# Expert tiles as float16 pairs in a kernel that joins a delta-rule attention and a mixture of experts

## The chip, the cores and the metric

The kernel runs on one core of one Trainium2 chip. The metric is the device time of the whole program in microseconds (us), lower is better. A core has five engines with instruction streams of their own: TensorE (PE in the profile, its weight loads PEld), VectorE (DVE), ScalarE (ACT), GpSimd (POOL) and SyncE (SP), and 16 DMA engines that they share. [...]

## The reference

The input x is 2 batches of 2048 rows of 256 numbers, float32. What is computed:

```
xn = layernorm(x)                                  # rows of 256
q, k, v, g = xn@Wq, xn@Wk, xn@Wv, xn@Wg            # 4 heads, DK = 128, DV = 64
k = k / |k| ; q = q * DK**-0.5 ; beta = sigmoid(xn@Wb)
S_t = S_{t-1} + k_t (beta_t (v_t - k_t^T S_{t-1}))^T ;  o_t = q_t^T S_t    # per batch and head
s = (rmsnorm(o) * norm_w * silu(g)) @ Wo
e = argmax(softmax(xn @ router_w^T))               # one of 8 experts for each row
h = relu(xn @ expert_fc[e])**2                     # 1024 wide
y = h @ expert_proj[e]^T                           # 256 wide
out = x + s * silu(y)
```

## The kernel before, in words

**The recurrence.** Each batch is cut into 16 chunks of 128 rows. A chunk is worked on for both batches b and all heads together. `K`, `Q` and `VG` project it, with both operands held as pairs of float16 numbers (high and low part), three matmuls for each product. From k come its transpose (`kT`), the product `G`, and from that X, the strictly upper part of a 128 by 128 matrix for each head (`X32`, `X_h`, and `X_l` on GpSimd). The inverse of the unit triangle 1 + X is built in six levels: each level is `L` and `Dm` and `T` on TensorE, with `Pm_` and `dM` on VectorE and `dZ` on ScalarE between them, for b = 0 and b = 1 in turn. M and Z are the inverse and its transpose. `MZ` and `Zo` on VectorE and `M0` on TensorE set them up: `MZ` copies the identity into M, and `M0` then writes its even columns. At the end of the levels `F`, `Fr_` and `Zc` correct the inverse by one Newton step; `Fr_` adds `ImM`, which is identity minus M and comes from GpSimd. Then `KS`, `U`, `O` and `dS` carry the state S from chunk to chunk, and `ogT_` and `wo` finish the rows.

**The experts.** The 4096 rows are sorted by expert into NT = 39 tiles of 128 rows, a tile having one expert. For a tile, `load_weights` on SP fetches both weight matrices, 1 MB each in float32, into one of three buffers (RING = 3): tile j is fetched once tile j-3 is done. `rows` on GpSimd gathers the rows, TensorE transposes them, and `expert_tile` multiplies: 16 matmuls of 128 columns, then relu and square on ScalarE (`relu`, `sq`), then 8 matmuls of 256 columns. All of that is float32. A float32 matmul stands in the trace as two instructions. `keep_y`, `y_sigmoid`, `gate_y` and `send_y` finish a tile and scatter it into a DRAM scratch, y_d.

**The order.** Nothing is scheduled at run time. Each engine has its order written out by hand: `ramp` (normalisation, routing, the first chunk and its first three tiles), then a step for each chunk i, which holds the levels of chunk i, the state of chunk i-1 and the projections of chunk i+1 with two or three expert tiles dealt out between them by `experts(n)`: seven steps with three tiles (`step3`, i = 1 to 7), five with two (`step2`, i = 8 to 12), and `tail` for chunks 13 to 15 and the last five tiles. `experts(n)` issues n sixteenths of a tile. At the end y_d is read back (wts<-y_d), and `weigh` and `add_x` make the output.

The order of one level and its neighbours in `step2`, for TensorE:

```
L(i, 4) ; wo(i - 1) ; Dm(i, 4) ; experts(2) ; T(i, 4) ; experts(1) ; L(i, 5) ; experts(1) ; Dm(i, 5) ; experts(1)
```

Lines that the rows name: L509 and L520 are the matmuls of an expert tile (`expert_tile`), L539, L555 and L589 are `K`, `Q` and `VG`, L614 is `M0`, L629, L638 and L647 are `L`, `Dm` and `T`, L659, L660 and L668 are `F` and `Zc`, L731 is `wo`, L483 to L485 are the three products of a pair. L1164 is `sq`, L1132 a step of splitting the attention's weights, L1728 is `q_l`, L1768 the identity copy of `MZ`, L2440 is `k_l`, L2446 is `X_l`, L2466 is `ImM_`. L372 is SP's load of the first half of x for the output.

## Time and profile before

| | |
|---|---|
| median of 3 runs (lowest to highest) | 783.77 us (781.04 to 786.33) |
| the profiled execution, its own time | 784.05 us |
| its span, first to last instruction | 782.3 us |
| busy: PE, DVE, POOL, ACT | 722.2, 542.5, 396.9, 354.2 us |
| mean granted TensorE clock | 0.994 of full speed |
| moved by DMA | 116.33 MB |

Busy time of TensorE counts an instruction from its start to its modelled end, and instructions overlap. What an instruction costs the engine is therefore read from the distance between the starts of neighbours. The span divides into a ramp, up to the start of step 3 at 213 us, five steps of three tiles, five of two tiles, and a tail. From step 2 on, one step with three tiles follows the other at a distance of 47.67 us; the steps with two tiles follow at 40.17 us.

### The profile page before, as it was taken

Reading aid. Unit: us, or ns where it says so; the run is one execution under the profiler, and the core shown is the slowest. Engines: PE = TensorE matmul, PEld = TensorE weight load, DVE = VectorE, ACT = ScalarE, POOL = GpSimd, SP = SyncE. Lnnn points to the kernel's source line nnn. Section 1 sums busy time; section 2 is a strip of 40 time slices with the busy share of each in tenths; the row PEclk is TensorE's granted clock in tenths of the full one; section 3 lists DMA queues with packets and bytes.
Section 4 is the critical chain, followed back from the end, with each engine's and each line's share of the span. In section 5 each row is a group of like instructions: output and inputs, shape, how many; then the busy total and the mean of one; then the engine's idle time right before and its main releaser. Section 6 shows DMA issues by size and latency. Waiting matters only on the chain.

```text
span 782.3 us, 23109 instructions
## 1 busy us (share of the span) xinstructions
PE 722.2 (92%) x9442; PEld 621.6 (79%) x9442; DVE 542.5 (69%) x1169; ACT 354.2 (45%) x768; POOL 396.9 (51%) x411
## 2 busy tenths in 40 slices
PE   5666899999999999999999999999999999999976
PEld 4555798878889788887888878888888887979853
DVE  4779457566575665756556577877777777787788
ACT  5551354445444454444445344444444453545432
POOL 3571538354473545626454354647464646545351
PEclk9998999999999999999999999999999999999999
DMA  9420973452335434343354333333333323323076
GB/s 300 145 83 1 386 287 143 153 213 116 130 129 197 162 115 176 134 177 130 116 204 152 131 130 116 128 115 126 116 129 116 129 116 129 131 108 103 22 232 220
DMA packets 37753, 116.33 MB, mean 149 GB/s; under 512 B 3664, under 2 KB 24400, under 8 KB 27664
## 3 DMA queue, kind: packets, MB, share of 16 engines
q1 hardware_dynamic: 33904, 104.62, 36.7%
q0 software_dynamic: 3744, 10.23, 3.9%
q8 instruction: 76, 1.25, 0.7%
q14 instruction: 29, 0.24, 0.1%
HBM read 101.33 MB, written 13.50 MB: 147 GB/s over the span
## 4 chain that ended last, share of the span: by engine, by line
PE 68%; DVE 13%; POOL 7%; issue 6%; DMA 3%; ACT 2%; SPq 0%; DVEq 0%; POOLq 0%
PE bank L509 17%; PE bank L520 16%; PE bank L589 4%; PE bank L483 4%; PE bank L485 3%; PE bank L484 3%; PE bank L555 3%; PE bank L629 2%; PE bank L647 2%; PE bank L638 2%; PE bank L731 2%; PE bank L539 2%; POOL XTl L2446 2%; PE bank L568 2%; DVE M L1768 2%
## 5 line engine op out<-in xcount | busy, mean ns | idle before, releaser
L520 PE MATMUL bank<-wts,hT 128*128 128x256 f32 x624 | 170.9, 393 | 0.0
L509 PE MATMUL bank<-xsT,wts 128*128 128x128 f32 x1248 | 166.0, 281 | 1.2 <-DMA wts<-in_pj 1.1
L509 PEld LDWEIGHTS bank<-xsT,wts 128*128 128x128 f32 x1248 | 150.6, 192 | 4.7 <-DMA wts<-in_pj 1.2
L1785 DVE TENSOR_TENSOR Pm<-bank,lvl_mask 128x256 f16<-128x256 f32 x180 | 68.1, 417 | 62.6 <-PE bank L629 61.9
L520 PEld LDWEIGHTS bank<-wts,hT 128*128 128x128 f32 x624 | 105.4, 191 | 7.3
L2446 POOL TENSOR_TENSOR XTl<-f_t,XTh 128x512 f16<-128x512 f32 x32 | 40.0, 1257 | 125.6 <-DVE XTh L1723 125.4
L1215 ACT CAST Z<-bank 128x256 f16<-128x256 f32 x180 | 59.3, 376 | 96.7 <-PE bank L647 96.6
L1796 DVE TENSOR_TENSOR M<-bank,M 128x256 f16<-128x256 f32 x180 | 68.8, 418 | 38.7 <-PE bank L638 37.8
L1160 ACT ACTIVATE hT<-bank 128x512 f32<-128x512 f32 x78 | 46.7, 599 | 46.9 <-PE bank L509 46.9
L2466 POOL TENSOR_TENSOR ImM<-ident,M 128x512 f32<-128x512 f16 x30 | 35.1, 1189 | 42.1 <-DVE M L1796 42.1
L555 PE MATMUL bank<-xT,wq 128*128 128x128 f16 x768 | 49.3, 222 | 4.1 <-DVE qT16l L1728 3.6
L555 PEld LDWEIGHTS bank<-xT,wq 128*128 128x128 f16 x768 | 45.8, 99 | 5.8 <-issue 3.9
L1164 ACT ACTIVATE hT<-hT 128x512 f32<-128x512 f32 x78 | 49.3, 632 | 1.1
L2440 POOL TENSOR_TENSOR k16l<-f_t,k16h 128x512 f16<-128x512 f32 x32 | 38.1, 1205 | 20.4 <-DVE k16h L1709 20.4
L2419 POOL TENSOR_TENSOR y_sb<-y_sb,y_sg 128x256 f32<-128x256 f32 x39 | 29.5, 757 | 36.5 <-ACT y_sg L1179 36.3
L589 PE MATMUL bank<-wvg,xT 128*128 128x512 f16 x192 | 46.7, 379 | 0.7 <-DVE qT16l L1728 0.7
L539 PE MATMUL bank<-wk,xT 128*128 128x512 f16 x192 | 46.2, 379 | 1.0 <-DVE xT L1609 1.0
L2423 POOL DMA_INDIRECT y_d<-y_sb,to_row x39 | 41.1, 1053 | 8.6 <-issue 5.7
L1768 DVE COPY M<-ident 128x512 f16<-128x512 f16 x30 | 26.7, 889 | 26.4 <-PE bank L485 25.2
L2410 POOL DMA_INDIRECT xs<-xn_d,from_row x39 | 40.5, 1037 | 6.8 <-issue 5.6
L2397 POOL TENSOR_TENSOR root<-beta,up_half 128x8 f32<-128x8 f32 x16 | 29.1, 1821 | 28.5 <-DVE gate L1743 16.2
L1716 DVE TENSOR_TENSOR f_t<-bank,up_neg 128x512 f32<-128x512 f32 x32 | 21.8, 684 | 30.6 <-PE bank L485 30.6
(257 smaller groups left out, 1975.5 us busy)
## 6 DMA issues: line engine op xcount, KB each, us to landing
wts<-in_fc SPq DMA_DIRECT2D x39, 1024.0 KB, 4.9
wts<-in_pj SPq DMA_DIRECT2D x39, 1024.0 KB, 8.4
wts<-in_x SPq DMA_DIRECT2D x10, 512.0 KB, 8.2
wts<-y_d SPq DMA_DIRECT2D x4, 1024.0 KB, 9.6
out_x<-wts SPq DMA_DIRECT2D x16, 256.0 KB, 2.8
xn_d<-wts SPq DMA_DIRECT2D x3, 1024.0 KB, 4.4
x_first<-in_x SPq DMA_DIRECT2D x4, 512.0 KB, 16.4
wts<-in_x SPq DMA_DIRECT2D x4, 256.0 KB, 3.5
```

Of the source, the lines that this page charges most:

```text
L509: ins = pe.matmul(psum[bank[n]][:, (c % 4) * P:(c % 4 + 1) * P], fcw[r][:, k, c * P:(c + 1) * P], xsT[:, k, :], start=(k == 0), stop=(k == ...
L520: ins = pe.matmul(psum[bank[0]][:, 0:D], hT[:, c, :], pjw[r][:, c, :], start=(c == 0), stop=(c == HC - 1))
L539: ins = pe.matmul(psum[KG_BANK[b]][:], xT[:, a, zx, b, k, :], wk16[:, zw, k, :], start=(k == 0 and zx + zw == 0), stop=(k == KC - 1 and zx ...
L555: ins = pe.matmul(bank4(QV_BANK)[:, h, :], wq16[:, zw, k, h * DK:(h + 1) * DK], xT[:, a, zx, b, k, :], start=(k == 0 and zx + zw == 0), st ...
L589: ins = pe.matmul(psum[QV_BANK][:], xT[:, a, zx, b, k, :], wvg16[:, zw, k, :], start=(k == 0 and zx + zw == 0), stop=(k == KC - 1 and zx = ...
L1160: act.activation(half(n), psum[H_BANK[j % 2 ^ n]][:], ACT.Relu).then_inc(relu_ok[n], 1)
L1164: act.activation(half(n), half(n), ACT.Square).then_inc(sq_ok[n], 1)
L1215: act.copy(evens(h4(Zs[last(m)], b), s, 1), half4(level_bank(m, b)).rearrange("p h (n c) -> p h n c", c=s)).then_inc((last_dZ_ok if last(m ...
L1768: dve.tensor_copy(h4(Ms[last(m)], b), ident16[:].unsqueeze(1).to_broadcast([P, H, P]))
L1785: dve.tensor_tensor(h4(Pms[last(m)], b).rearrange("p h (n c) -> p h n c", c=s), half4(level_bank(m, b)).rearrange("p h (n c) -> p h n c", ...
L1796: dve.tensor_tensor(evens(h4(Ms[last(m)], b), s), half4(level_bank(m, b)).rearrange("p h (n c) -> p h n c", c=s), evens(h4(Ms[last(m)], b) ...
L2446: pool.tensor_tensor(h4(XT[1][a % 2], b), h4(f32_t, b), h4(XT[0][a % 2], b), ALU.subtract).then_inc(Xl_ok[b], 1)
```

## The change

1. **Tiles in float16 pairs.** From tile T16 = 9 on (30 of 39 tiles) each float32 product of an expert tile becomes three products of float16 halves: 48 matmuls of 128 columns and 24 of 256 columns. The rows are split when they are kept (ScalarE the high part, `rows_low` on VectorE the low one). After relu, ScalarE makes the high part of h by a square written as float16 (`h_high`) beside the float32 square (`sq`), and GpSimd the low part (`h_low`).
2. **Weights split once.** All expert weights are split during the ramp, in 32 units of 128 by 1024 numbers (512 KB in, 512 KB out). ScalarE issues the load, makes the high part and issues the store (`unit_load`, `unit_high`, `unit_store`), VectorE makes the low part (`unit_low`); the result is in a DRAM scratch w16_d, from which tiles 9 to 38 are fetched, again 1 MB twice. Two units are under way at a time, in the space of x_first. SP therefore loads the first half of x for the output only when all units are stored, right before the fetch for tile 9.
3. **The unit triangle.** `X32` writes by a predicated copy into a tile `unit` that holds the identity, so X comes with its diagonal; `F` then yields M + XM, and `Fr_` is identity minus that, with no `ImM_`. `P32` no longer waits for `X_l`.
4. **M0 whole.** `M0` multiplies by the whole identity (128 columns for each head where there were 64), `M0c` keeps all of it, and the identity copy of `MZ` is gone.
5. **New orders.** The ramp now holds chunks 0 to 2 and nine tiles; `step3` runs for chunks 3 to 7, `step2` for 8 to 12, and every order is written anew.

```diff
-        FIRST_TILES, STEPS = 3, [3] * 7 + [2] * 5
+        FIRST_TILES, FIRST_STEP, STEPS = 9, 3, [3] * 5 + [2] * 5
...
+        w16_d = scratch("w16_d", [E, P, 2, 2, KC * HD], F16)
...
                 def load_weights(j):
                     ex = sp.value_load(tile_e[0:1, j:j + 1], min_val=0, max_val=E - 1)
+                    if j >= T16:
+                        for m in range(2):
+                            sp.dma_start(w16[j % RING][:, m], w16_d[bass.ds(ex, 1), :, m].rearrange("a p z n -> p (a z) n")
+                                         ).then_inc(wt_in[j % RING], 16)
+                        return
...
-                sp.wait_ge(wl_ok, len(W_ORDER))
+                for j in range(RING, T16):
+                    At(sp, j - RING).on(yp)
+                    load_weights(j)
+                for z in range(2):
+                    sp.wait_ge(unit_kept[z], 16 * UNITS // 2)
                 xf = x_first.rearrange("p c (b d) -> p b c d", b=B)
...
-                for j in range(RING, NT):
+                for j in range(T16, NT):
...
+                            else:
+                                ins = pairs(o, [fcw16[r][:, z, k, c * P:(c + 1) * P] for z in range(2)],
+                                            [xsT16[:, z, k, :] for z in range(2)], start=(k == 0), stop=(k == KC - 1))
...
+                        for zh in range(2):
+                            for c in range(HC):
+                                if c % 4 == 0 and zh == 0:
+                                    pe.wait_ge(hh_ok[c // 4], HH_FROM[c // 4] + j - T16 + 1)
+                                if c % 4 == 0 and zh == 1:
+                                    pe.wait_ge(hl_ok[c // 4], HL_FROM[c // 4] + j - T16 + 1)
+                                for zw in range(2 - zh):
...
+                                    ins = pe.matmul(psum[bank[0]][:, 0:D], h16[:, zh, c, :], pjw16[r][:, zw, c, :],
+                                                    start=(n == 0), stop=(n == 3 * HC - 1))
...
-                            ins = pe.matmul(half4(level_bank(m, b))[:, h, :], Zs[last(m)][:, H * b + h, :],
-                                            evens(ident16[:].unsqueeze(1), 1)[:, 0].rearrange("p n c -> p (n c)"),
+                            ins = pe.matmul(bank4(level_bank(m, b))[:, h, :], Zs[last(m)][:, H * b + h, :], ident16[:],
                                             start=True, stop=True)
...
+                def unit_load(u):
+                    if u < 2:
+                        act.wait_ge(wl_ok, W_ORDER[("wk", "wq")[u]])
+                    else:
+                        act.wait_ge(unit_lo, u - 1)
+                    act.dma_start(unit_in[u % 2], unit_of(u)[0]).then_inc(unit_read[u % 2], 16)
+
+                def unit_high(u):
+                    act.wait_ge(unit_read[u % 2], 16 * (u // 2 + 1))
+                    if u < 2:
+                        act.wait_ge(wl_ok, W_ORDER[("wbr", "wvg")[u]])
+                    else:
+                        act.wait_ge(unit_kept[u % 2], 16 * (u // 2))
+                    act.activation(unit_out[u % 2][:, 0], unit_in[u % 2], ACT.Copy, scale=W_SCALE).then_inc(unit_hi, 1)
+
+                def unit_store(u):
+                    act.wait_ge(unit_lo, u + 1)
+                    act.dma_start(unit_of(u)[1], unit_out[u % 2]).then_inc(unit_kept[u % 2], 16)
...
+                def h_high(j, n):
+                    At(act, j).on(relu_ok[n])
+                    act.activation(h16[:, 0, 4 * n:4 * n + 4, :].rearrange("p c n -> p (c n)"), half(n), ACT.Square,
+                                   scale=H_SCALE).then_inc(hh_ok[n], 1)
...
+                def unit_low(u):
+                    dve.wait_ge(unit_hi, u + 1)
+                    dve.scalar_tensor_tensor(out=unit_out[u % 2][:, 1], in0=unit_in[u % 2], scalar=W_SCALE,
+                                             in1=unit_out[u % 2][:, 0], op0=ALU.mult, op1=ALU.subtract).then_inc(unit_lo, 1)
+
+                def rows_low(j):
+                    if T16 <= j < NT:
+                        At(dve, j).on(xsT_ok)
+                        dve.tensor_tensor(xsT16[:, 1].rearrange("p k n -> p (k n)"), psum[H_BANK[j % 2]][:, 0:KC * P],
+                                          xsT16[:, 0].rearrange("p k n -> p (k n)"), ALU.subtract).then_inc(xsl_ok, 1)
...
-                    dve.tensor_tensor(h4(f32_t, b), bank4(KG_BANK[b]), up_neg[:].unsqueeze(1).to_broadcast([P, H, P]),
-                                      ALU.mult).then_inc(X32_ok[b], 1)
+                    fr.on(Gp[b])
+                    fr.on(Xl_ok[b], Xh_ok[b], back=1)
+                    dve.copy_predicated(h4(unit, b), up_strict[:].bitcast(I32).unsqueeze(1).to_broadcast([P, H, P]),
+                                        bank4(KG_BANK[b])).then_inc(X32_ok[b], 1)
...
+                def h_low(j, n):
+                    At(pool, j).on(sq_ok[n])
+                    pool.wait_ge(hh_ok[n], HH_FROM[n] + j - T16 + 1)
+                    cs = slice(4 * n, 4 * n + 4)
+                    pool.tensor_tensor(h16[:, 1, cs, :], hT[:, cs, :], h16[:, 0, cs, :], ALU.subtract).then_inc(hl_ok[n], 1)
...
-                def ImM_(m, b):
```

Three places of the new orders follow, each before and after.

**TensorE, from level 0 of a step with three tiles.** Before, the second product of a tile (`wts,hT`, 256 columns, float32), level products and `Q` of the next chunk:

```order
L629 MATMUL bank<-M,XTh 128x64 x8
L520 MATMUL bank<-wts,hT 128x256 x4
L638 MATMUL bank<-Pm,Z 128x64 x8
L520 MATMUL bank<-wts,hT 128x256
L555 MATMUL bank<-xT,wq 128x128 x24
```

Now the same part of the first such step, where the second product is on float16 halves (`wts,h`):

```order
L566 MATMUL bank<-wts,h 128x256 x3
L687 MATMUL bank<-M,XTh 128x64 x8
L614 MATMUL bank<-xT,wq 128x128 x24
L566 MATMUL bank<-wts,h 128x256 x3
L696 MATMUL bank<-Pm,Z 128x64 x8
```

`Q` stands between `L` and `Dm` now, and each piece of a tile is three short matmuls.

**GpSimd, in a step with three tiles.** Before: `k_l`, gathers (L2410), `X_l`, gating of y (L2419), `ImM_` (L2466), scatters (L2423), `P_l` (L2452):

```order
L2440 TENSOR_TENSOR k16l<-f_t,k16h 128x512 x2
L2410 DMA xs<-xn_d,from_row 128x256
L2446 TENSOR_TENSOR XTl<-f_t,XTh 128x512 x2
L2410 DMA xs<-xn_d,from_row 128x256
L2419 TENSOR_TENSOR y_sb<-y_sb,y_sg 128x256 x2
L2423 DMA y_d<-y_sb,to_row 4480x256
L2466 TENSOR_TENSOR ImM<-ident,M 128x512 x2
L2397 TENSOR_TENSOR root<-beta,up_half 128x8
L2419 TENSOR_TENSOR y_sb<-y_sb,y_sg 128x256
L2423 DMA y_d<-y_sb,to_row 4480x256 x2
L2452 TENSOR_TENSOR PTl<-f_t,PTh 128x512 x2
```

Now, from the gating of the step's first tile on:

```order
L3040 TENSOR_TENSOR y_sb<-y_sb,y_sg 128x256
L3034 TENSOR_TENSOR h<-hT,h 128x512 x3
L3040 TENSOR_TENSOR y_sb<-y_sb,y_sg 128x256
L3034 TENSOR_TENSOR h<-hT,h 128x512
L3025 DMA xs<-xn_d,from_row 128x256
L3073 TENSOR_TENSOR PTl<-f_t,PTh 128x512
L3040 TENSOR_TENSOR y_sb<-y_sb,y_sg 128x256
L3067 TENSOR_TENSOR XTl<-unit,XTh 128x512
L3073 TENSOR_TENSOR PTl<-f_t,PTh 128x512
L3044 DMA y_d<-y_sb,to_row 4480x256 x2
L3067 TENSOR_TENSOR XTl<-unit,XTh 128x512
```

`h_low` (L3034) is new, six times in a step; `ImM_` is gone, and `X_l` (L3067) has moved to the end.

**ScalarE, in the ramp, around level 3 of chunk 0.** Before, relu (L1160) and square (L1164) of a tile, `dZ` (L1215), `kTc` (L1191):

```order
L1215 CAST Z<-bank 128x16x16 x2
L1204 ACTIVATE gate<-bank 128x256
L1160 ACTIVATE hT<-bank 128x512
L1164 ACTIVATE hT<-hT 128x512
L1191 COPY kT_1<-bank 128x1024
L1160 ACTIVATE hT<-bank 128x512
```

Now:

```order
L1440 CAST Z<-bank 128x16x16
L1349 DMA w_d<-x_first 128x2x1024
L1375 ACTIVATE hT<-bank 128x512
L1337 DMA x_first<-in_fc 128x1024
L1375 ACTIVATE hT<-bank 128x512
L1440 CAST Z<-bank 128x16x16
L1429 ACTIVATE gate<-bank 128x256
L1349 DMA w_d<-x_first 128x2x1024
L1385 ACTIVATE hT<-hT 128x512
```

Stores (L1349) and loads (L1337) of units stand between the copies that the levels wait for; each of them, and each `unit_high` (L1345), waits for something of its own.

## Rows read from the trace of the kernel before

**Rows 1.** The page, part 1: busy us, share of the span, instructions of each engine.
```profile
PE 722.2 (92%) x9442; PEld 621.6 (79%) x9442; DVE 542.5 (69%) x1169; ACT 354.2 (45%) x768; POOL 396.9 (51%) x411
```

**Rows 2.** Stretches: length; busy us (instructions) of PE, PEld, DVE, ACT, POOL; clock, DMA share, GB/s.
```profile
87.00:213.00 126.00, 123.30 (x1511) 109.24 (x1512) 74.83 (x161) 58.91 (x130) 62.06 (x62) 1.00 0.52 195
213.10:260.80 47.70, 46.22 (x599) 40.53 (x597) 29.88 (x64) 21.83 (x49) 24.20 (x25) 1.00 0.43 150
494.60:534.80 40.20, 39.55 (x547) 33.93 (x546) 31.01 (x65) 18.66 (x42) 23.07 (x21) 1.00 0.35 122
651.70:744.70 93.00, 89.67 (x1288) 79.35 (x1286) 70.55 (x154) 43.08 (x99) 46.63 (x46) 1.00 0.29 102
744.70:782.30 37.60, 27.20 (x317) 17.46 (x312) 32.02 (x54) 11.18 (x23) 13.35 (x12) 0.97 0.71 235
```

**Rows 3.** TensorE in order of time: start us, us, engine, line, operation, count.
```profile
524.12 1.97 PE L731 MATMUL bank<-wo_sb,ogT 128*128 128x256 f32 x8
525.93 0.40 PE L638 MATMUL bank<-Pm,Z 128*128 128x64 f16 x8
526.16 1.11 PE L520 MATMUL bank<-wts,hT 128*128 128x256 f32 x4
...
533.90 1.58 PE L509 MATMUL bank<-xsT,wts 128*128 128x128 f32 x12
535.32 1.46 PE L539 MATMUL bank<-wk,xT 128*128 128x512 f16 x6
536.62 0.61 PE L509 MATMUL bank<-xsT,wts 128*128 128x128 f32 x4
...
538.29 1.50 PE L555 MATMUL bank<-xT,wq 128*128 128x128 f16 x24
539.63 1.46 PE L539 MATMUL bank<-wk,xT 128*128 128x512 f16 x6
```

**Rows 4.** Groups by line and shape: operation, count, busy us, mean ns, idle before.
```profile
L1164 ACT ACTIVATE hT<-hT 128x512 f32<-128x512 f32 x78 | 49.3, 632 | 1.1
L2440 POOL TENSOR_TENSOR k16l<-f_t,k16h 128x512 f16<-128x512 f32 x32 | 38.1, 1205 | 20.4 <-DVE k16h L1709 20.4
L2466 POOL TENSOR_TENSOR ImM<-ident,M 128x512 f32<-128x512 f16 x30 | 35.1, 1189 | 42.1 <-DVE M L1796 42.1
L1768 DVE COPY M<-ident 128x512 f16<-128x512 f16 x30 | 26.7, 889 | 26.4 <-PE bank L485 25.2 <-POOL lvl_mask L2332 1.2
L1728 DVE SCALAR_TENSOR_TENSOR qT16l<-bank,qT16h 128x512 f16<-128x512 f32 x32 | 21.8, 682 | 1.5 <-ACT qT16h L1198 1.5
L1735 DVE SCALAR_TENSOR_TENSOR v_sb<-bank,root 128x256 f32<-128x256 f32 x32 | 13.2, 413 | 0.5 <-ACT gate L1204 0.5
L1132 ACT ACTIVATE x_first<-x_first 128x1024 f32<-128x1024 f32 x3 | 3.2, 1054 | 4.7 <-DMA x_first<-in_wk 4.7
L1768 DVE COPY wk<-ident 128x512 f16<-128x512 f16 x2 | 0.9, 436 | 0.0
```

**Rows 5.** The chain of waits in a step with two tiles: start us, us, what.
```profile
522.98 2.84 POOL XTl L2446 x2
...
529.66 2.46 POOL ImM L2466 x2
```

**Rows 6.** DMA from 0 to 213 us: a queue's packets, MB, share; issues, KB, us to landing.
```profile
q1 hardware_dynamic: 15216, 35.41, 45.9%
...
wts<-in_x SPq DMA_DIRECT2D x6, 512.0 KB, 8.5
...
x_first<-in_x SPq DMA_DIRECT2D x4, 512.0 KB, 16.4
```

**Rows 7.** SP's queue in order of time, 76 to 100 us: start, us, what.
```profile
77.62 0.37 SPq L356 DMA_DIRECT2D wts<-in_fc  x1
...
82.45 13.09 SPq L372 DMA_DIRECT2D x_first<-in_x  x4
```

**Rows 8.** The chain that ended last, in the tail: start us, us, what.
```profile
749.23 5.47 DMA wts<-y_d
```

More of the change, by code:

```diff
@@ new lines, in ramp @@
+                    dZ(1, 0, 1)
+                    unit_high(19)
+                    unit_high(20)
+                    relu(3, 1)
+                    sq(3, 1)
+                    dZ(1, 1, 0)
+                    dZ(1, 1, 1)
+                    unit_store(19)
+                    unit_load(21)
+                    keep_rows(4)
+                    keep_y(3)
+                    unit_store(20)
+                    unit_load(22)
+                    kTc(2, 0)
+                    q_h(2, 1)
@@ new lines, in ramp @@
+                    unit_high(26)
+                    ksq_(3, 1)
+                    M0c(2, 0)
+                    M0c(2, 1)
+                    relu(6, 1)
+                    ksq_(3, 0)
+                    unit_load(28)
+                    unit_high(27)
+                    sq(6, 1)
+                    osq(1)
+                    unit_store(26)
+                    unit_load(29)
+                    q_h(3, 0)
+                    y_sigmoid(5)
+                    dZ(2, 0, 1)
+                    dZ(2, 0, 0)
@@ new lines, in ramp @@
+                    keep_rows(7)
+                    unit_store(27)
+                    keep_y(6)
+                    unit_high(28)
+                    relu(7, 0)
+                    q_h(3, 1)
+                    sq(7, 0)
+                    dZ(2, 1, 1)
+                    unit_load(30)
+                    dZ(2, 1, 0)
+                    relu(7, 1)
+                    unit_store(28)
+                    unit_high(29)
+                    sq(7, 1)
+                    unit_store(29)
+                    kTc(3, 1)
@@ new lines, in ramp @@
+                    dZ(2, 2, 1)
+                    unit_load(31)
+                    y_sigmoid(6)
+                    dZ(2, 2, 0)
+                    keep_rows(8)
+                    unit_high(30)
+                    kTc(3, 0)
+                    unit_store(30)
+                    unit_high(31)
+                    keep_y(7)
+                    dZ(2, 3, 0)
+                    dZ(2, 3, 1)
+                    relu(8, 0)
+                    unit_store(31)
+                    sq(8, 0)
@@ L2533, in step3 @@
+                    X_l(3, 1)
+                    send_y(7)
+                    send_y(8)
                 def step3(i, t):
-                    rows(t + 2)
                     krn_(i + 1)
+                    h_low(t, 0)
+                    h_low(t, 1)
                     orn_(i - 1)
@@ L2558, in step2 @@
                     rows(t + 2)
+                    h_low(t, 1)
+                    h_low(t, 0)
+                    k_l(i + 1, 0)
+                    k_l(i + 1, 1)
+                    h_low(t + 1, 0)
                     orn_(i - 1)
                     ogm(i - 1)
[L2561 to L2567 removed]
```

1896 lines of the change are left out of this document (1210 added, 686 removed).

## The prediction, made before the changed kernel ran

> **What bounds the kernel now.** I read the page first: TensorE is busy for 92% of the span, VectorE for 69%, GpSimd for 51%, ScalarE for 45% [rows 1]. An average over stages with different limits doesn't say which one binds, so next come the stretches [rows 2]. In a step with three tiles TensorE is busy 46.2 of 47.7 us, in one with two tiles 39.55 of 40.2, in the ramp from 87 to 213 us 123.3 of 126. VectorE has 29.9, 31.0 and 74.8 there. The steps and the later ramp are bound by TensorE, and a tile costs its own TensorE time: the two kinds of step differ by one tile and 7.5 us. The last 37.6 us are another stage: VectorE is busy for 32.0 of them [rows 2], and the chain runs through the read of y_d [rows 8]. No expert tile is left there, so the change can only shift it.
>
> What TensorE pays for an instruction is the distance between starts [rows 3]. Float32 with 128 columns: 12 instructions from 533.90 to 535.32, 0.118 us each. Float32 with 256 columns: 8 from 524.12 to 525.93, 0.226 each. Float16 with 128 columns: 24 from 538.29 to 539.63, 0.056 each. With 512: 6 from 535.32 to 536.62, 0.217 each. With 64: 8 from 525.93 to 526.16, 0.029 each. [...]
>
> **The tiles.** Before, 32 x 0.118 + 16 x 0.226 = 7.4 us. After, 48 x 0.056 = 2.7, and 24 matmuls of 256 columns in float16, which no row shows: a third of the way from 128 to 512 columns, in proportion, gives 0.110 each, 2.6 in all. That is 5.3 us, so a tile saves 2.1 us; the bounds of the unseen instruction, 0.108 (half of 0.217) and 0.113 (half of 0.226), move this by 0.1. For 30 tiles it is 63 us of TensorE. M0 with twice the columns costs 8 x 0.027 = 0.2 us a chunk.
>
> **Steps with three tiles, five of them.** TensorE: -6.3 + 0.2 = -6.1 us. Is the rest small enough to stay beside 41.6 us? VectorE: 29.9, less two identity copies of 0.89 [rows 4], plus three `rows_low` like the 256-wide read of PSUM at 0.41 [rows 4], 29.3. ScalarE: 21.8 + 6 x 0.63 for `h_high` [rows 2, 4] and under 0.5 for the wider `M0c`, 26. GpSimd: 24.2 + 6 x 1.2 - 2 x 1.19 [rows 2, 4], 29. All are hidden by TensorE as long as each result is there when its matmul is reached. I give back 0.6 us a step for results that are late (0 to 1.5): -5.5 each, -27.5 together.
>
> **Steps with two tiles, five of them.** TensorE: -4.2 + 0.2 = -4.0. VectorE: 31.0 - 1.8 + 0.8 = 30.0 of 36.2 us, 83% where it was 77%. GpSimd, 23.1 + 4.8 - 2.4 = 25.5, is on the chain of these steps today with `X_l` and `ImM_` [rows 5]; the one moves off it and the other is gone, and if `h_low` comes late it takes their place, in front of the last third of a tile's second product. I give back 0.8 us (0 to 2.5): -3.2 each, -16 together.
>
> The predicated copy of `X32` is in no row. Below it can't be under the 0.44 us of a 512-wide copy within SBUF [rows 4], above I take twice the 0.68 of a 512-wide read of PSUM [rows 4]; I take 0.68, since it too reads PSUM, and so no change. For 32 of them the bounds are -8 to +22 us of VectorE, beside TensorE's work; they are in what I give back and in the range.
>
> **The tail.** Up to 744.7 us TensorE is busy 89.7 of 93, with five tiles: -10.5 + 0.6. VectorE has 70.6 of 93, with the levels of two chunks nested at the end. I take half of it, -5 (0 to -10). Behind it the last 37.6 us stay.
>
> **The ramp.** Here the change only adds. A unit costs ScalarE 1.05 us for the high part [rows 4] and two issues, VectorE the low part: 1024 wide, at most twice 0.68, I take 1.3. An issue costs 0.37 us, or 13.09 / 4 = 3.3 when the queue is backed up [rows 7]. By the new order of VectorE seven low parts stand ahead of the routing's end, so 25 units are left for the stretch from 87 to 213 us. There VectorE gets 74.8 + 25 x 1.3 - 6 x 0.89 = 102 us and ScalarE 58.9 + 25 x (1.05 + 0.74) = 104 us of 126 [rows 2]: full, and no longer far from TensorE. The DMA engines: 195 GB/s for 126 us are 24.6 MB [rows 2]; less the 2.1 MB of x that now load later, plus 25 x 1.05 MB, 48.7 MB. At the rate at which they worked when busy, 35.41 MB in 45.9% of 213 us or 362 GB/s [rows 6], that takes 134 us: up to 8 us over, or nothing if the fetches for tiles 10 and 11 slip behind the step's start. By the turn of a buffer: half a megabyte lands after 8.5 us [rows 6], then high and low part, and the next load starts while the store runs: 8.5 + 2.35 = 10.9 us for two units, 12.5 turns, 136 us, 10 us over. Against that stand some 4 us in which the routing comes ahead of chunk 0's triangle and the identity copies. I take +6 (-4 to +25).
>
> [...]
>
> **The sum.** -27.5 - 16 - 5 + 6 = -42.5 us. Against the profiled execution's own 784.05 us (its span is 782.3; the median of the runs is 783.77, so the two agree) that is **741 us**.
>
> **Rivals.**
> *Another engine becomes the bound of the steps.* The same identity copy takes 436 ns in the last chunk and 889 on average before it [rows 4], and nothing but the work beside it differs: VectorE is held up at times by GpSimd. `h_low` adds 4 to 6 operations of 1.2 us to GpSimd in a step. Some 14 operations of VectorE in a step work within SBUF; if half of them lose 0.45 us more, that is 3.2 us a step; the 0.6 to 0.8 us given back above already hold a part, and the rest, 2.2 us over ten steps, adds 22: 741 + 22 = 763 us. Against it: TensorE hides 77% of busy VectorE today with hardly a gap. 14%. [...]
>
> *The units stall ScalarE: slower than before.* ScalarE is in order, and each `unit_high` waits for a load and an older store while the relu, `dZ` and `kTc` behind it, and so TensorE's levels and tiles, wait too. The price is 12.5 turns of landing time L plus 2.35 us, less 126. At 16.4 us, which the same 512 KB took while three tiles were fetched beside them [rows 6], it is +108 and the kernel takes 843 us. It decides from L = 11.6 us on, where it eats the 48.5 us of steps and tail, and from 12.2 us the kernel is slower by over 1%. For it: tiles are fetched beside the units all through the ramp. Against it: at 16.4 us 8 MB were queued at once, and here at most a tile and two units are. 9%, and 6% for an L just short of that, which ends within 1% (776 to 791 us).
>
> *TensorE alone counts.* Everything is on time, the ramp loses nothing, the tail gives all: 784 - 30.5 - 20 - 10 - 4 = 719 us. 7%.
>
> The forecast, steps as worked out and a ramp that costs little, has 64%.
>
> **The numbers.** From 717 to 774 us lie the forecast, the first rival and most of the last; left out are the slow ramp, what ends near the old time, and what lies below 717, together under 20%. About 1% (8 us) can be told from no change. Faster by over that: 64 + 14 + 7 = 85%; within it 6%; slower 9%.
>
> **What would show it.** Neighbouring starts of 0.11 us for the 256-wide float16 matmuls; steps 42.2 and 37.0 us apart instead of 47.67 and 40.17, read from K of one chunk to K of the next; step 3 starting at 219 us; a unit's load landing after about 9 us; VectorE at some 30 us in both kinds of step. I am wrong if TensorE's busy share in the steps falls below 90% (the first rival), if step 3 starts after 240 us or ScalarE's waits for loads of units sum to tens of us (the second), or if tile 9's weights, queued behind x, hold TensorE at the start of step 3 for over 5 us.

## The result, and the profile after

The changed kernel takes **822.13 us** (median of 4 runs, 817.96 to 827.6), the kernel before 783.56 beside it: 1.049 times as long, 95% interval 1.046 to 1.052. The forecast was 741 us, 10% below what was measured. The profiled execution took 827.6 us, its span is 825.9, so it stands 43.6 us above the span before. It is the longest of the four runs, 5.5 us above their median, so what is read from it below is a few us too large against the medians.

The page first (part 1, then TensorE's busy tenths and its granted clock in 40 slices of 20.6 us each):

```profile
PE 701.4 (85%) x10162; PEld 597.8 (72%) x10162; DVE 597.3 (72%) x1199; ACT 420.3 (51%) x860; POOL 442.2 (54%) x440
PE   5784678769779988989988888999999999989984
PEclk9897789889989999999999999999999999999996
```

Against [rows 1], TensorE is busy 21 us less while the kernel is 44 us longer. The holes in its row lie in the first third, and there the clock is down too.

To see where the time went, take the same point of each chunk, the start of K: start us, us, engine, line, what, count. Of the changed kernel, K of chunks 4, 5, 9 and 14:

```profile
272.04 1.46 PE L598 MATMUL bank<-wk,xT 128*128 128x512 f16 x6
317.44 1.46 PE L598 MATMUL bank<-wk,xT 128*128 128x512 f16 x6
511.75 2.51 PE L598 MATMUL bank<-wk,xT 128*128 128x512 f16 x6
695.28 1.03 PE L598 MATMUL bank<-wk,xT 128*128 128x512 f16 x4
```

And of the kernel before, chunks 4, 9 and 14:

```profile
213.76 1.46 PE L539 MATMUL bank<-wk,xT 128*128 128x512 f16 x6
453.94 1.46 PE L539 MATMUL bank<-wk,xT 128*128 128x512 f16 x6
654.42 1.46 PE L539 MATMUL bank<-wk,xT 128*128 128x512 f16 x6
```

| stretch | before | after | difference | forecast |
|---|---|---|---|---|
| ramp, up to K of chunk 4 | 213.8 | 272.0 | +58.3 | +6 |
| five steps of three tiles, K 4 to K 9 | 240.2 | 239.7 | -0.5 | -27.5 |
| five of two tiles, K 9 to K 14 | 200.5 | 183.5 | -17.0 | -16 |
| tail, K 14 to the end | 127.9 | 130.6 | +2.7 | -5 |

The differences add up to 43.5 us, the difference of the spans but for rounding. Three terms of the sum failed: the ramp by 52 us, the three-tile steps by 27, the tail by 8. Some of the ramp's 58 us belong to this one execution: in the profiles of runs 4, 5 and 6 below, whose ramp has the same order, K of chunk 4 starts at 265.1 to 266.7 us and not at 272.0.

**The ramp.** Stretches of the changed kernel, with the columns of [rows 2]: four pieces of the ramp, the three-tile steps, one step with two tiles, the tail in two pieces:

```profile
0.00:80.20 80.20, 49.47 (x573) 42.23 (x574) 62.72 (x157) 44.25 (x73) 32.70 (x61) 0.87 0.85 284
80.20:151.90 71.70, 49.17 (x477) 40.24 (x478) 38.05 (x66) 27.05 (x50) 23.80 (x20) 0.82 0.69 233
151.90:211.40 59.50, 47.33 (x525) 39.15 (x524) 30.77 (x54) 28.06 (x53) 17.69 (x17) 0.93 0.76 263
211.40:272.00 60.60, 54.81 (x633) 47.10 (x630) 39.95 (x76) 30.22 (x61) 28.58 (x27) 0.92 0.65 218
271.00:510.00 239.00, 213.72 (x3363) 186.93 (x3360) 169.11 (x328) 127.42 (x274) 146.32 (x141) 0.96 0.45 166
549.10:585.75 36.65, 35.03 (x595) 30.55 (x593) 30.74 (x65) 21.10 (x45) 24.81 (x24) 1.00 0.37 131
692.70:788.00 95.30, 88.19 (x1495) 75.82 (x1494) 79.22 (x165) 51.88 (x115) 62.68 (x59) 0.98 0.31 104
788.00:825.90 37.90, 24.87 (x220) 15.54 (x220) 26.18 (x46) 8.72 (x17) 10.78 (x6) 0.82 0.69 226
```

From 80 to 152 us no engine is full: VectorE has 38 of 71.7 us, ScalarE 27, the DMA engines 69%. That is a stretch bound by waiting, not by work. ScalarE's waits from 50 to 271 us (us in total, times, longest) and SP's one wait for the last unit:

```profile
ACT x_first L1345 <- DMA w_d<-x_first: 16.6, 3, 6.7
ACT x_first L1345 <- DMA x_first<-in_fc: 12.6, 3, 6.2
ACT x_first L1345 <- issue: 11.4, 1, 11.4
ACT x_first L1345 <- DMA x_first<-in_pj: 8.0, 3, 4.3
SPq L402 <- DMA w_d<-x_first: 41.5, 1, 41.5
```

`unit_high` (L1345) waits for the store of unit u-2 (the first row) and for its own load. The median transfer is quick; from issue to landing, up to 271 us:

```profile
w_d<-x_first ACTq DMA_DIRECT2D x32, 512.0 KB, 5.0
x_first<-in_fc ACTq DMA_DIRECT2D x16, 512.0 KB, 6.3
```

The medians hide the few that count. Of the 32 loads four took 10.6 to 12.1 us, of the 32 stores three 10.4 to 11.2. ScalarE stands in front of the missing unit, and what TensorE needs stands behind it in ScalarE's stream, here `hT` (L1385, the square of a tile):

```profile
146.74 1.06 ACT L1345 ACTIVATE x_first<-x_first 128x1024 f16<-128x1024 f32 x1 [6.19 <-DMA x_first<-in_fc]
149.16 1.22 PE L579 MATMUL bank<-wts,hT 128*128 128x256 f32 x2 [6.22 <-ACT hT L1385]
PE bank L579 <- ACT hT L1385: 16.5, 3, 6.2
```

The last row is TensorE's waits from 80 to 271 us. There are three, 6.2, 5.7 and 4.5 us, and each comes 1.6 to 2.4 us after a `unit_high` that waited for a transfer of 10.4 to 11.2 us (a load landing at 146.7 us, stores landing at 175.5 and 231.1). Behind each of them the granted clock stays at 0.50 of full speed for another 3 to 6 us.

**The three-tile steps.** TensorE at the end of level 3 of step 3 and at the start of step 4 (rows in order of time; in brackets the idle time before and what ended it):

```profile
296.45 0.49 PE L566 MATMUL bank<-wts,h 128*128 128x256 f16 x3
299.53 0.44 PE L526 MATMUL bank<-ident,xs 128*128 128x128 f32 x2 [2.59 <-DMA xs<-xn_d,from_row]
...
318.74 1.50 PE L614 MATMUL bank<-xT,wq 128*128 128x128 f16 x24
323.16 0.19 PE L517 MATMUL bank<-R_h,Z 128*128 128x64 f16 x1 [2.92 <-DVE R_l L2268]
...
323.85 2.35 PE L598 MATMUL bank<-wk,xT 128*128 128x512 f16 x6
325.99 0.31 PE L517 MATMUL bank<-xsT,wts 128*128 128x128 f16 x1
...
327.75 0.22 PE L519 MATMUL bank<-xsT,wts 128*128 128x128 f16 x1
327.81 0.22 PE L517 MATMUL bank<-xsT,wts 128*128 128x128 f16 x1
```

From K of chunk 4 to K of chunk 9 TensorE has five gaps of 1.2 to 2.6 us that wait for gathered rows, one in each step, four of 2.9 us that wait for `R_l`, and one of 2.1 us for `xsT` at the end. Behind the gap at 323.16 the six matmuls of K take 2.14 us to their successor where the same six took 1.30 at 317.44, and the next 16 take 1.7 us where 0.9 would do: from 324.3 to 327.7 us the granted clock is 0.50 of full speed, and 1.00 from 317.4 to 318.7 us. So this gap of 2.9 us costs another 1.7. The clock fell like this behind seven of the ten gaps. Why the rows come late is GpSimd's order (start, us; the gather, and what stands ahead of it):

```profile
284.04 1.16 POOL L3034 TENSOR_TENSOR h<-hT,h 128x512 f16<-128x512 f32 x1
286.00 1.16 POOL L3034 TENSOR_TENSOR h<-hT,h 128x512 f16<-128x512 f32 x1 [0.80 <-ACT hT L1385]
...
291.84 1.06 POOL L3025 DMA_INDIRECT xs<-xn_d,from_row  x1 [0.16 <-issue]
```

It is issued at 291.84 behind both `h_low` of the step's first tile, and its rows arrive 7.65 us later; TensorE had come to the transpose at 296.9.

**What the operations cost.** Groups of the changed kernel by line and shape, with the columns of [rows 4]:

```profile
L3034 POOL TENSOR_TENSOR h<-hT,h 128x512 f16<-128x512 f32 x60 | 72.5, 1212 | 129.7 <-ACT hT L1385 129.6
L2131 DVE SCALAR_TENSOR_TENSOR x_first<-x_first 128x1024 f16<-128x1024 f32 x32 | 41.7, 1306 | 37.6 <-ACT x_first L1345 37.6
L1345 ACT ACTIVATE x_first<-x_first 128x1024 f16<-128x1024 f32 x32 | 33.9, 1059 | 51.2 <-DMA w_d<-x_first 16.6 <-DMA x_first<-in_fc 12.6 <-issue 11.4
L2173 DVE CAST XTh<-unit 128x512 f16<-128x512 f32 x32 | 28.8, 926 | 0.0
L2207 DVE CAST PTh<-f_t 128x512 f16<-128x512 f32 x32 | 23.8, 744 | 0.2
L2166 DVE COPY_PREDICATED unit<-up_strict,bank 128x512 f32<-128x512 int32 x32 | 22.3, 728 | 3.0 <-PE bank L519 3.0
```

The prices of the new instructions are near the forecast: `unit_low` 1.31 us (forecast 1.3), `unit_high` 1.06 (1.05), `h_low` 1.21 (1.2), the predicated copy 0.73 (0.68). What the sum had no term for are the two old casts (L2173 is `X_h`, L2207 is `P_h`). Before they were:

```profile
L1757 DVE CAST PTh<-f_t 128x512 f16<-128x512 f32 x32 | 16.8, 527 | 0.0
L1723 DVE CAST XTh<-f_t 128x512 f16<-128x512 f32 x32 | 13.1, 426 | 0.1
```

The means hide two kinds. In the changed kernel 29 of these 64 casts have no GpSimd instruction beside them (under 0.1 us of one) and take 406 to 429 ns; the other 35 take 1.18 us on average and up to 2.80. In every three-tile step, right ahead of `R_l`, one `X_h` takes 2.8 us and one `P_h` 1.27, so VectorE loses 3.2 us there, and at four of the five places TensorE waits 2.9.

### The profile page after: what moved, and what is told of

It reads as the page before. It is cut to its first block, busy times and chain, and to the rows that moved or that the text cites. A ratio compares the mean times of both kernels' runs of the same rounds, so it can differ in the third digit from the quotient of the medians.

```text
span 825.9 us, 24858 instructions
## 1 busy us (share of the span) xinstructions
PE 701.4 (85%) x10162; PEld 597.8 (72%) x10162; DVE 597.3 (72%) x1199; ACT 420.3 (51%) x860; POOL 442.2 (54%) x440
## 4 chain that ended last, share of the span: by engine, by line
PE 50%; DVE 18%; DMA 15%; issue 7%; ACT 4%; POOL 3%; SPq 1%; POOLq 1%; ACTq 1%; DVEq 0%
PE bank L566 7%; DMA xs<-xn_d,from_row 6%; PE bank L517 5%; PE bank L519 5%; PE bank L518 5%; PE bank L648 4%; PE bank L614 4%; DMA w_d<-x_first 3%; DMA x_first<-in_fc 3%; PE bank L705 2%; PE bank L696 2%; PE bank L579 2%; PE bank L687 2%; PE bank L598 2%; PE bank L627 2%
## 5 line engine op out<-in xcount | busy, mean ns | idle before, releaser
L3034 POOL TENSOR_TENSOR h<-hT,h 128x512 f16<-128x512 f32 x60 | 72.5, 1212 | 129.7 <-ACT hT L1385 129.6
L566 PE MATMUL bank<-wts,h 128*128 128x256 f16 x720 | 106.2, 276 | 0.1
L517 PE MATMUL bank<-xsT,wts 128*128 128x128 f16 x480 | 88.0, 222 | 2.1 <-DVE xsT L2137 2.1
L518 PE MATMUL bank<-xsT,wts 128*128 128x128 f16 x480 | 87.8, 222 | 0.0
L519 PE MATMUL bank<-xsT,wts 128*128 128x128 f16 x480 | 87.7, 222 | 0.0
L566 PEld LDWEIGHTS bank<-wts,h 128*128 128x128 f16 x720 | 64.7, 99 | 9.3 <-POOL h L3034 0.6
L2131 DVE SCALAR_TENSOR_TENSOR x_first<-x_first 128x1024 f16<-128x1024 f32 x32 | 41.7, 1306 | 37.6 <-ACT x_first L1345 37.6
L3040 POOL TENSOR_TENSOR y_sb<-y_sb,y_sg 128x256 f32<-128x256 f32 x39 | 33.6, 861 | 65.9 <-ACT y_sg L1404 65.9
L3025 POOL DMA_INDIRECT xs<-xn_d,from_row x39 | 40.7, 1044 | 44.3 <-DVE to_row L2126 28.6
L1375 ACT ACTIVATE hT<-bank 128x512 f32<-128x512 f32 x78 | 46.6, 599 | 34.9 <-PE bank L519 25.7
L1345 ACT ACTIVATE x_first<-x_first 128x1024 f16<-128x1024 f32 x32 | 33.9, 1059 | 51.2 <-DMA w_d<-x_first 16.6
L579 PE MATMUL bank<-wts,hT 128*128 128x256 f32 x144 | 42.9, 420 | 16.6 <-ACT hT L1385 16.5
L598 PE MATMUL bank<-wk,xT 128*128 128x512 f16 x192 | 52.9, 418 | 1.1 <-DVE f_t L2200 1.1
L517 PEld LDWEIGHTS bank<-xsT,wts 128*128 128x128 f16 x480 | 47.9, 100 | 4.2 <-issue 3.0
L1385 ACT ACTIVATE hT<-hT 128x512 f32<-128x512 f32 x78 | 49.1, 629 | 1.2 <-DVE x_first L2131 0.7
L518 PEld LDWEIGHTS bank<-xsT,wts 128*128 128x128 f16 x480 | 47.8, 100 | 2.1 <-issue 0.8
```

Source lines behind the costliest of these rows:

```text
L517: pe.matmul(outp, lhs[0], rhs[0], start=start, stop=False)
L518: pe.matmul(outp, lhs[0], rhs[1], start=False, stop=False)
L519: return pe.matmul(outp, lhs[1], rhs[0], start=False, stop=stop)
L566: ins = pe.matmul(psum[bank[0]][:, 0:D], h16[:, zh, c, :], pjw16[r][:, zw, c, :], start=(n == 0), stop=(n == 3 * HC - 1))
L579: ins = pe.matmul(psum[bank[0]][:, 0:D], hT[:, c, :], pjw[r][:, c, :], start=(c == 0), stop=(c == HC - 1))
L598: ins = pe.matmul(psum[KG_BANK[b]][:], xT[:, a, zx, b, k, :], wk16[:, zw, k, :], start=(k == 0 and zx + zw == 0), stop=(k == KC - 1 and zx ...
```

## The experiments

Names: A is the theory that the units' transfers and ScalarE's waits in order stretch the ramp, B that the units' arithmetic does, C and E that the ramp's new order costs time by itself, F that the DMA engines' rate sets the pace of the units, S that the three-tile steps lose to the two gaps, D that VectorE bounds those steps. All ratios are to the kernel before, run on the same chip, with their 95% intervals.

**1. Four units in place of 32.**

```diff
 def unit_load(u):      # unit_high, unit_store and unit_low likewise
+    if u >= 4:
+        return
...
-    w16_d[bass.ds(ex, 1), :, m]
+    w16_d[0:1, :, m]
```

> Only the first 4 of the 32 units are loaded, split and stored (they lie ahead of 48 us); every float16 tile then fetches expert 0's pair, 1 MB twice as before, so the results of other experts are wrong. All orders stay. Theory A (the units' transfers: ScalarE waits in order for their landings, and gathers and weights land late beside them): the three-tile steps start at 213 to 220 us instead of 271, and the kernel takes 822 - 55 = 767 us (760 to 775). Theory B (the units' arithmetic fills ScalarE and VectorE): the same here. Theory C (the new order of the ramp is slow by itself): step 3 still starts after 250 us and the kernel takes over 800.

Measured: 783.31 us, ratio 1.001 [0.998, 1.003]. K of chunk 4 starts at 232.4 us. That is between A's range and C's, so both hold a part. Of the 58 us, 40 are the other 28 units, 1.4 us each (39 by the medians of the whole time); 18 are left without them. The last two pieces of this kernel's ramp:

```profile
127.50:173.70 46.20, 44.29 (x526) 38.07 (x525) 24.27 (x52) 21.53 (x48) 17.92 (x19) 1.00 0.40 147
173.70:232.40 58.70, 52.68 (x634) 45.33 (x630) 34.02 (x68) 23.58 (x53) 24.45 (x25) 0.94 0.48 165
```

The first of them, 46.2 us long, is about what a chunk with three tiles costs undisturbed; the other takes 12 us more.

**2 and 3. Arithmetic without transfers, transfers without arithmetic.**

```diff
 def unit_load(u):      # run 2; unit_store likewise
+    if u >= 4:
+        return
```

```diff
 def unit_high(u):      # run 3; unit_low likewise
+    n = UNIT if u < 4 else 8
-    act.activation(unit_out[u % 2][:, 0], unit_in[u % 2], ...)
+    act.activation(unit_out[u % 2][:, 0, 0:n], unit_in[u % 2][:, 0:n], ...)
```

> From the fifth unit on the high and low parts are still made by ScalarE and VectorE in their places, but no unit is loaded or stored (28 of 32; every float16 tile fetches expert 0's pair). Theory A: within 12 us of the kernel with four units, 767 to 780 us. Theory B: most of the loss is back, 800 to 822 us.

> From the fifth unit on all loads and stores run with their waits, but the high and low parts are made of 8 columns instead of 1024 (the rest of the stored unit is stale). Theory A: 800 to 822 us, step 3 starts after 250 us. Theory B: 775 to 790 us.

Measured: 793.17 us (1.014 [1.009, 1.018]) and 798.01 us (1.018 [1.013, 1.023]). In run 2 a high part waits for the low part two units back in place of a load and a store. Beside the 783.3 with four units, arithmetic alone costs 10 us and transfers alone 15; both together cost 39. Neither time lies in A's range or in B's. So neither is right by itself: 14 us come only where both are there. Each unit is then a chain of load, high, low and store through queues that are in order; that this chain is the reason is read from the waits above.

**4. Both edits of the three-tile steps.**

```diff
                 def step3(i, t):        # GpSimd
                     krn_(i + 1)
+                    rows(t + 2)
                     h_low(t, 0)
...
                     k_l(i + 1, 1)
-                    rows(t + 2)
                     rows(t + 3)
...
                     P32(i + 1, 1)       # VectorE, end of step3
+                    P_h(i + 1, 1)
+                    rows_low(t + 3)
+                    R32(i)              # where the next step began with them
+                    R_h(i)
+                    R_l(i)
                     X_h(i + 1, 1)
                     X_h(i + 1, 0)
-                    rows_low(t + 3)
-                    P_h(i + 1, 1)
```

> Two edits in the three-tile steps only. On GpSimd the gather of tile t+2 is issued after krn_, ahead of h_low, orn_, ogm and k_l. On VectorE R32, R_h and R_l of the next step stand ahead of the two X_h, and P_h ahead of rows_low. Theory S (the step loses to a gather that is issued 7 us before its rows are needed, to U waiting for R_l behind X_h and P_h, and to the half clock after each of these two gaps): distance of the three-tile steps from 47.3 to 42 to 43.5 us, kernel 822 - 5 x 4.5 = 800 us (795 to 806). [...]

Measured: 804.26 us (1.027 [1.023, 1.030]), 18 less than the changed kernel. From K of chunk 4 to K of chunk 9 it is 220.7 us where it was 239.7. One such step, with a granted clock of 1.00 throughout:

```profile
307.80:351.90 44.10, 40.71 (x671) 35.84 (x668) 34.60 (x66) 24.93 (x55) 28.59 (x29) 1.00 0.45 162
```

S holds. D, by which the distance would have stayed above 46 us and the kernel above 815 us, fails. TensorE's 40.7 us are near the 40.1 that the prediction's terms give (46.2 - 6.1). The step is still 3.4 us longer than that. In the five steps TensorE waits for VectorE's `R_l` (4.3 and 3.9 us, two places) and `Z` (3.7) and for GpSimd's `h` (2.3), none of them above 1.0 us; one wait of 1.8 us for `xsT` ends the last step. The granted clock stays at 1.00 behind all of these. Ahead of `R_l` VectorE has this in each step:

```profile
350.71 2.70 DVE L2207 CAST PTh<-f_t 128x512 f16<-128x512 f32 x1
```

The same cast takes 0.42 us at 348.26. From 350.25 to 353.12 us GpSimd runs three instructions nearly without a pause (a gather's issue, `P_l`, a gating), and the cast ends at 353.41. It loses 2.3 us, and TensorE's wait for this `R_l` is 0.96.

**5 and 6. Each edit alone.**

> Only the gather of tile t+2 is moved, to right behind krn_, in the three-tile steps; VectorE's order is the changed kernel's. Theory S: one of the two gaps of a step goes with its half clock, so about half of the 18 us that both edits gave: 812 to 815 us. Rival: the two gaps hide each other, and one alone gives under 3 us (over 819).

> Only VectorE's order at the end of the three-tile steps is changed (R32, R_h, R_l of the next step ahead of the two X_h); the gather stays late. Theory S: 4 to 8 us less than the changed kernel, 814 to 818 us. Rival: the late gather takes over the whole wait, 820 to 823 us.

Measured: 807.12 us with the gather alone (1.030 [1.026, 1.034]), 818.58 with VectorE's order alone (1.045 [1.042, 1.047]): 15.0 and 3.6 us less than 822.1, together close to the 18 of both. Between K 4 and K 9 they take off 15.4 and 6.4 us, both edits 19.0. They hardly hide each other. The gather's is the larger part, more than the half that was expected, and VectorE's order alone gave just less than the 4 to 8 us expected.

**7. Scatters earlier in the ramp.**

```diff
                     send_y(3)
+                    send_y(4)
...
                     gate_y(5)
+                    send_y(5)
                     k_l(3, 0)
                     gate_y(6)
-                    send_y(4)
-                    send_y(5)
```

> Both edits of the steps, and on GpSimd in the ramp send_y(4) right behind send_y(3) and send_y(5) right behind gate_y(5), where they stood behind gate_y(6). Theory E (part of what the new order costs by itself is the scatter of tile 4, which keep_y of tile 7 waits for): 6 us less than with both edits of the steps, 798 us (795 to 801). Rival: the units' waits are in that place anyway, and nothing changes, 804 us.

Measured: 806.18 us (1.027 [1.022, 1.032]), no gain over 804.26, so the rival holds. In the run with four units TensorE waits 3.7 us in that place, for `keep_y` on ScalarE; with all units it waits 2.1 us there with both edits of the steps and 2.0 us with the early scatters too. With all units the scatters aren't what holds it.

**8 and 9. A third buffer.**

```diff
 unit_out = [stage[:, UNIT * n:UNIT * (n + 1)]... for n in (3, 2)]
+    + [h16[:].rearrange("p z c n -> p z (c n)")]
...
-    act.wait_ge(unit_kept[u % 2], 16 * (u // 2))
+    act.wait_ge(unit_kept[u % 3], 16 * (u // 3))
```

> As with the early sends, and h16, free until tile 9, is a third buffer for split units, so unit_high waits for the store of unit u-3 and no longer u-2. Theory A (waits for the units' landings in ScalarE's order): the 16.6 us of ScalarE's waits for stores go, 10 to 15 us less, 785 to 789 us. Rival F (the DMA engines' rate sets the pace, so the wait moves to the loads): 796 to 800 us.

> As with the early sends, but three buffers for loaded units and two for split ones, and each load is issued one unit earlier. Theory A: the 21 us of waits for loads go, 10 to 20 us less, 780 to 789 us. Rival F: 796 to 800 us.

Measured: 790.77 us with three buffers for split units (1.008 [1.005, 1.012]), 15 less than 806.18; 800.57 with three for loaded ones (1.020 [1.015, 1.024]), 6 less. The first lies just above A's range and well below F's, the second in F's. Of the two hand-overs the store of unit u-2 held the ramp more. With the loads a unit earlier, the wait moves: ScalarE's waits for stores are then 17.4 and 5.6 us where they were 16.6.

**10. The old order in the ramp, four units.** All four engines follow the order of the kernel before for the ramp and for steps 1 and 2, with `ImM_` left out and the first units dealt in.

```diff
                 def ramp():          # TensorE; ScalarE, VectorE and GpSimd likewise
...
-                    KS(0)
                     M0(0)
...
                     F(0)
-                    experts(1)
+                    experts(8)
                     Zc(0)
-                    experts(4)
-                    U(0)
+                    KS(0)
+                    K(2, 0)
+                    experts(6)
+                    U(0)
```

> The order of the kernel before (its ramp and its steps 1 and 2) in place of the new ramp, on all four engines, with the new instructions in it, only 4 of 32 units (as in the run with four units: every float16 tile fetches expert 0's pair), and both edits of the three-tile steps. Theory E (the new order of the ramp costs 19 us by itself): step 3 starts at 213 to 220 us instead of 232, and the kernel takes 783 - 18 (both edits of the steps) - 15 = 750 us (745 to 758). Rival: the extra waits of the new instructions cost the 19 us in any order, 765 us.

Measured: 756.16 us (0.964 [0.961, 0.968]). K of chunk 4 starts at 218.1 us, where it was 232.4. E holds with 14 us. The last piece of its ramp, against the 58.7 us above:

```profile
170.50:218.10 47.60, 46.34 (x602) 40.69 (x599) 29.75 (x62) 22.17 (x49) 22.14 (x23) 1.00 0.54 195
```

The whole change, with both edits of the steps, is worth 28 us where the weights are nearly free.

**11. All units in the old order**, one every 5.1 us, three buffers for split ones.

```diff
                     unit_high(9)         # ScalarE, level 3 of chunk 0
                     keep_rows(1)
                     keep_y(0)
                     unit_load(11)
                     unit_store(9)
                     dZ(0, 3, 0)
```

> The same old order with all 32 units in it, one every 5.1 us from 78 us on, dealt out by the times of the kernel before, three buffers for split units, both edits of the three-tile steps. Theory A with E: the units still cost 20 us (what they cost with three buffers), the order's 15 are back: 770 to 776 us, below the kernel before. Rival F (the DMA engines carry units and tiles at no more than their mean rate of the ramp, 67.9 MB in 271 us): the ramp is no shorter than with the new order, 785 to 792 us.

Measured: 786.03 us (1.002 [1.000, 1.004]). A's range is missed and F's is met, but the trace shows a hold-up that F doesn't name. Its execution is the fastest of ten (780.7 us), with K of chunk 4 at 237.6. The first three-tile step takes 49.8 us, the next three 44.2. TensorE's one wait there, and SP's queue:

```profile
PE bank L517 <- DMA wts<-w_d: 7.4, 1, 7.4
```
```profile
234.59 2.04 SPq L406 DMA_DIRECT2D x_first<-in_x  x4
237.38 5.28 SPq L383 DMA_DIRECT2D wts<-w_d  x6
```

2 MB of x are queued ahead of tile 9's weights. It is the hold-up that the prediction named as its last condition, though the changed kernel itself doesn't show it, since its TensorE comes later.

**12 and 13. x later; and the float16 tiles from tile 12 on.**

```diff
-                xf = x_first...      # ahead of the fetch for tile 9
...
                 for j in range(T16, NT):
                     load_weights(j)
+                    if j == T16 + 2:
+                        xf = x_first...
```

```diff
-T16 = 9
+T16 = 12
-FIRST_TILES, FIRST_STEP, STEPS = 9, 3, [3] * 5 + [2] * 5
+FIRST_TILES, FIRST_STEP, STEPS = 12, 4, [3] * 4 + [2] * 5
```

> The run with paced units, and SP's load of the first half of x for the output stands behind the fetch for tile 11, where it stood ahead of the fetch for tile 9. Theory G (in the first three-tile step, 49.8 us long where the next are 44.2, TensorE waits for the weights of tile 9, queued behind 2 MB of x): the step goes to 45 us and the kernel to 786 - 5 = 781 us (779 to 783). Rival: the fetch for tile 9 waits for the last unit's store, which x doesn't change: under 1.5 us less, 785 us.

> As the run before it, but tiles 9 to 11 stay float32 (T16 = 12): the old order also for step 3, and the 32 units are dealt out over one more step, one every 5.7 us. Theory A (what binds the units is how many must pass beside the tiles in so short a stretch): the float32 step costs 47.7 - 44.2 = 3.5 us, the fetch for tile 12 no longer waits, and of the 25 us that units and late weights cost together 12 to 15 go: 770 to 776 us, faster than the kernel before. Rival H (each unit has its price, wherever it stands): 781 + 3.5 = 785 us.

Measured: **778.27 us** with x later (0.992 [0.990, 0.994]): theory G holds, with 7.8 us where 5 were expected. The first three-tile step takes 42.8 us where it took 49.8. This version beats both kernels, the one before by 0.8%, little but clear of the noise. From tile 12 on it is 779.91 (0.995 [0.993, 0.997]), 1.6 us more than its neighbour. A's 770 to 776 was wrong; H would give 778.3 + 3.5 = 781.8, so at most 2 us of the units' price went with the longer stretch. The ramp of the run with x later:

```profile
75.80:138.00 62.20, 50.86 (x497) 42.02 (x496) 38.50 (x67) 29.52 (x54) 19.64 (x17) 0.84 0.87 317
138.00:191.40 53.40, 48.31 (x601) 40.42 (x598) 41.53 (x72) 31.37 (x60) 26.84 (x25) 1.00 0.90 322
191.40:243.80 52.40, 48.85 (x602) 42.43 (x599) 39.55 (x71) 29.36 (x58) 23.11 (x23) 0.97 0.72 232
```

K of chunk 4 at 243.8 us is 25.7 later than with four units in this order, 0.9 us for each of 28; the medians of the whole time are 22.1 us apart, 0.8 each. In the new order with three buffers it is about the same: 790.8 - (783.3 - 18) = 25.5 us, where 783.3 - 18 is an estimate for four units with both edits of the steps. So a unit's price has two parts, 0.8 to 0.9 us that neither the order, nor the third buffer, nor the longer stretch took away, and 0.5 us that went with the third buffer.

## Why the prediction was wrong, step by step

- **TensorE's prices: right.** Three float16 matmuls of 256 columns take 0.33 us to their successor (0.110 each, as forecast), 128 columns 0.055. A three-tile step has 40.7 us of busy TensorE in the run with both edits; the prediction's terms give 40.1.
- **Steps with two tiles: right.** Forecast 37.0 us apart, measured 36.7 (five distances of 36.1 to 37.35); -17.0 us against -16. TensorE is busy for 35.0, VectorE for 30.7 (forecast 30.0).
- **Steps with three tiles: "I give back 0.6 us" was mis-sized.** It was 6 us a step: the steps came out at 47.9 us on average, 0.1 less than the 48.0 before, where the sum had taken 6.1 off for TensorE's work. The prediction checked that each engine's sum fits beside TensorE's and took punctuality for granted. The piece of GpSimd's new order that it showed begins with the gating of the first tile, behind the two `h_low` and the gather that decided. The runs showed in its place a gather issued too late and an `R_l` that comes late, with a granted clock of 0.50 behind seven of the ten gaps: moving the gather gave 15.0 us, moving `R_l` 3.6. The share of busy TensorE, 213.7 of 239 us or 89%, is below the 90% named as the mark of the first rival.
- **That rival, another engine becoming the bound, held in part.** VectorE's casts went from 0.43 to 0.93 us (`X_h`) and from 0.53 to 0.74 (`P_h`), 23 us over the kernel, and VectorE is busy for 33.9 us of a three-tile step where 29.3 were forecast. All of the casts' excess is in those with GpSimd instructions beside them. In the changed kernel they cost VectorE 3.2 us right ahead of the late `R_l`, in the run with both edits 2.3 us, so the gap that moving `R_l` shrank is largely this rival's (an estimate, by comparing the rows). As the bound of the step, which D stood for, it failed. What the trace shows is this: casts within SBUF with no GpSimd instruction beside them keep to 406 to 429 ns, the others take up to 2.80 us, and the predicated copies, which read PSUM, keep to 703 to 741 ns with or without one. By what the one engine holds up the other was not shown, and no run took GpSimd's operations away.
- **The ramp: +58 where +6 was forecast, the step that failed.** By the runs: 4 us in the old order with four units (218.1 against 213.8), 14 us for the new order, 40 for the other 28 units. The 4 us are there already at K of chunk 1 (73.7 against 69.4); that the first four units cost them, and not the new instructions, was not tried. The order was costed as a gain of 4 us, from where a few operations stand. The units were costed by three sums, each with all its resource to itself (VectorE 102 of 126 us, DMA 134, the turn of a buffer 136), and the largest taken. The step that failed is this: that the units' work on different engines overlaps, so that only its largest sum counts, and beside it a new order with no loss. The runs showed in its place 10 us for the arithmetic, 15 for the transfers and 39 for both, and 14 for the order.
- **The second rival, the units stall ScalarE: right in its mechanism, wrong in its condition.** Its marks came, step 3 after 240 us and ScalarE's waits for loads at 20.6 us (51.2 before `unit_high` in all). Yet it was to decide only from a landing time of 11.6 us, and the median landing took 5.0 to 6.3. The turn of two units was not 10.9 us but 15.6: 25 units took from the load at 60.4 to the last high part at 255.9. The price was put on an average turn. What the trace shows is that every load, high and low has a fixed place in a queue with relu, `dZ` and `kTc`, and that single transfers of 10.4 to 11.2 us are handed on whole, from ScalarE to TensorE's wait for `hT`. The rest of the turn is read from the orders, not from a run.
- **The price by bytes**, the prediction's 134 us for 48.7 MB at 362 GB/s, didn't decide here. From 80 to 272 us of the changed kernel the DMA engines are 65 to 76% busy; in the run with x later they are at 87 to 90% and 320 GB/s for 116 us. There the sum of the bytes may begin to bind, as theory F has it, and be a part of the 0.8 to 0.9 us; no run separates it from VectorE's 40 of 53 us.
- **The tail: nothing, where -5 was taken.** From K of chunk 14 to SP's read of y_d it is 95.1 us (94.8 before), and 2.5 us more than before lie behind that read. VectorE is busy for 79.2 of 95.3 there, 83%, before 76% [rows 2]. Whether VectorE or its waits hold it was not tried. From K 14 to the end it is 127.7 to 130.6 us in every run, with four units as with 32, so it owes little or nothing to the units.
- **Tile 9's weights behind x**: not in the changed kernel, but 7.4 us as soon as the ramp was faster.

## What to carry to other kernels

Sums of busy time tell whether work fits, not whether it is on time, and a median landing time hides the few late transfers that decide. Where orders are written by hand, follow the new order at each TensorE operation that waits for something far away (a gather, a store), and count back from it the landing time and what its queue holds ahead of it. Work that one feeds through several in-order queues can cost more than its longest part, here 39 us where the longest was 15; try one more buffer at the slowest hand-over early (it gave 15 us here). And measure the preparation and the new order apart from the gain: here the gain was 28 us, and both of them stood against it. Where VectorE and GpSimd work beside each other, read the longest of a group as well as its mean.

## What the runs showed of the hardware

- Gaps of 2 to 3 us brought TensorE's clock down here, though not always. Of the ten gaps of 1.2 to 2.9 us in the three-tile steps of the changed kernel the granted clock fell to 0.50 of full speed behind seven (1.95 to 2.92 us; three of them waits for gathered rows, three for `R_l` and one for `xsT`) and stayed at 1.00 behind three (1.19, 2.26 and 2.90 us). So the wait need not be for DMA: `R_l` and `xsT` come from VectorE. After the 2.92 us before `U` at 323.16, float16 matmuls of 128 columns came 0.107 us apart from 325.99 on and 0.055 from 327.7 on. In the mended steps the granted clock is 1.00, with waits up to 1.0 us and one of 1.8.
- Casts of VectorE within SBUF, 0.41 to 0.43 us with no GpSimd instruction beside them, took longer beside one instruction (`P_h` up to 1.34 us, though ten casts beside one kept to 0.41 to 0.42) and longest beside a row of them. In the run with both edits 0.42 us became 2.70 while GpSimd ran three, and the cast ended 0.3 us after the third. The five `X_h` of 2.79 to 2.80 us in the changed kernel end in the same way, 0.3 us behind three of them.
- A gather of 128 rows of 1 KB that GpSimd issues lands after 2.7 to 7.7 us in the steps; the one that TensorE waits for takes 6.3 to 7.7.
- The predicated copy of 128 by 512 numbers from PSUM takes 0.73 us; another read of PSUM of that size took 0.68 [rows 4].
